# Delta net stage of a six-stage kernel: block products that read the triangle itself, one relayed inverse turned on VectorE, and the inverse's chain of steps in four parts

## The chip, the cores and the metric

One Trainium2 chip, one of its cores. The metric is the device time of the whole program in microseconds, the median of several executions.

## The reference, cut to what matters

The program is a transformer piece of six stages in a row on an activation of 2 x 512 tokens x 256 channels: a mixture of experts with zero experts, an attention, the same mixture again, a mixture of eight experts with GELU, a gated delta net, and the GELU mixture again. The change touches the delta net only. For each of its 32 value heads and each chunk of 64 tokens the reference does this:

```python
decay_mask = jnp.exp(jnp.clip(g[..., :, None] - g[..., None, :], -30.0, 30.0))
decay_mask = decay_mask * jnp.tril(jnp.ones((chunk_size, chunk_size), jnp.float32))
attn = -(jnp.einsum('bhcid,bhcjd->bhcij', k_beta, k) * decay_mask)
attn = jnp.where(upper, 0.0, attn)
...
attn, _ = jax.lax.scan(_correct_row, attn, jnp.arange(1, chunk_size))
attn = attn + jnp.eye(chunk_size, dtype=attn.dtype)
value_corrected = jnp.einsum('bhcij,bhcjd->bhcid', attn, v_beta)
...
v_prime = v_c - jnp.einsum('bhld,bhde->bhle', kcd_c, state)
inter = jnp.einsum('bhld,bhde->bhle', q_c, state) * ge_c[..., None]
out = inter + jnp.einsum('bhij,bhjd->bhid', intra, v_prime)
new_state = state * gel_c[..., None] + jnp.einsum('bhld,bhle->bhde', k_c * kd_c, v_prime)
```

The row-by-row correction with the identity added is the inverse of a unit triangular 64 x 64 matrix. It must be had for each of 8 chunks x 2 sequences x 32 value heads before the chunk's new values can be formed; the state makes the chunks of a head a chain.

## The kernel before, in words

The delta net runs over 16 key heads (a "head" below), each with 2 value heads stacked on the 128 partitions. `run` (L1311) goes through one list of named steps, and every engine executes its own part of each step in that order: `prepare_order(0)`, `front_order(0, 0)` and one `pair_order` for the first head, then a loop of seven bodies of two heads (`body_order`), then one last body. Semaphore counts tie the engines together. So the order in which an engine does things is the written order, and a wait on one step holds up all that stands behind it on that engine.

A head has four pairs of chunks, and each is one call of `pair_order(done, build, front, extra)`. The call does three things side by side. It carries the state through the two chunks of `done`: `read_state` (PE L1527, L1531; DVE makes `wv`, L1879), `new_values` (PE L1546, ACT makes `vp`), `update` (PE L1560, L1564; DVE L1891 makes the new state, L1898 the output). It builds the inverses of the two chunks of `build` in two levels: `z` is a product (PE L1504) and a mask (DVE L1871, tile `zi`), `e` two products (PE L1513, L1517), copied out by ACT. And it makes the operands of the two chunks of `front`: `turn` (PE L1466, L1468), then `unit` for both chunks (POOL L1746 adds the identity to the chunk's triangle, `bi = ge + eye`) and `lower` (PE L1489: 16 products with the identity turn `bi`, ACT copies the result to `ai`). `z` takes `ai` as its stationary operand. `lower` stands at the end of a pair, right ahead of the next pair's `read_state`.

Between these fixed steps stand the `extra` slots 0 to 6, in which `body_order` (L1188) places the preparation of the next head q: the projections `proj` 0 to 11 (PE L1431, and L1438 for 8 to 11; alternately into PSUM banks A and C), the taps of a convolution (`tap`, DVE L1801 and L1804, 4 for each of 4 groups), `silu`, norms, `coefs`, `shares` (POOL L1739), and four times `gram` (PE L1478 into bank C) with `decay` (DVE L1841 and L1844, which empty bank C and write `intra` and the triangle `ge`). The call that has `done` = (j, 0) places norms and coefficients, (j, 2) the four grams, (j, 4) the rest, (j, 6) the output of head j and early work of head j + 2.

The starting blocks of the inverse, 16 x 16 each, come by a relay through DRAM. `spread` (SP L1379, L1383) stores the diagonal blocks of `ge` in 8 DMAs, waits, and loads them as `whole_blocks`, one block to a partition. `base` (DVE L1856 to L1864) inverts all blocks at once with a chain of 1 + 2 x 14 small instructions, each waiting for the one before, and a copy that turns the result. `gather` (SP L1387 to L1398) stores both results, waits for both, and issues 16 DMAs of 16 KB, 8 into `w16` and 8 into `w16t`, the inverse and its transpose in place for the products. `z` of level 0 waits for all of them (L1497), and the load of the next weights (`load_weights`, L1348, issued at `proj` 11) stands behind them in SP's order. These weights are needed by `proj` 0, slot 0 of the pair (j, 6).

```python
        yield from pair_order((j, 4), (j, 6), (q, 0) if prep else None, [
            SL("v1"), PR(8), PR(9), ONE("base") + ONE("gather") + PR(10), PR(11), [], []])
```

## Time and profile before

| | us |
|---|---|
| median of 3 runs (lowest, highest) | 3184.04 (3183.61, 3184.51) |
| the profiled execution | 3190.36 |
| its span, first to last instruction | 3188.6 |
| delta net, main loop and ends, in that span | 907 to 2783 |

The mean granted clock of TensorE over the span is 0.869 of full speed. The profile names the engines PE (TensorE; PEld is its weight load), DVE (VectorE), ACT (ScalarE), POOL (GpSimd) and SP (SyncE, which issues the DMAs). In a timeline a row is a group of equal instructions that follow each other: its start, its length, the engine, the line, what it writes and reads, how many; in brackets the engine's idle time before it and what ended that. "issue" is idle time in which no releaser was found.

### The profile page before, as it was taken

Reading aid. Unit: us, or ns where it says so; the run is one execution under the profiler, and the core shown is the slowest. Engines: PE = TensorE matmul, PEld = TensorE weight load, DVE = VectorE, ACT = ScalarE, POOL = GpSimd, SP = SyncE. Lnnn points to the kernel's source line nnn. Section 1 sums busy time; section 2 is a strip of 40 time slices with the busy share of each in tenths; the row PEclk is TensorE's granted clock in tenths of the full one; section 3 lists DMA queues with packets and bytes.
Section 4 is the critical chain, followed back from the end, with each engine's and each line's share of the span. In section 5 each row is a group of like instructions: output and inputs, shape, how many; then the busy total and the mean of one; then the engine's idle time right before and its main releaser. Section 6 shows DMA issues by size and latency. Waiting matters only on the chain. (4 is left out here: it accounts for less than half of the span.)

```text
span 3188.6 us, 60191 instructions
## 1 busy us (share of the span) xinstructions
PE 2620.2 (82%) x23890; PEld 1999.5 (63%) x23890; DVE 1616.2 (51%) x3376; ACT 1142.0 (36%) x2442; POOL 438.4 (14%) x479
## 2 busy tenths in 40 slices
PE   7899879999656778778778778777877877789998
PEld 4433559999534556556557556556655656679997
DVE  4443456766244445445455454454454544466663
ACT  1123222332134345445444444444444444323221
POOL 0011000000011122122122222222212212100000
PEclk9889889999768789789788788788888878889999
DMA  1000112010011110110110110010011000011110
GB/s 44 25 1 1 30 41 77 27 52 26 5 34 27 27 25 15 28 28 8 28 28 8 28 28 12 24 28 16 22 30 25 11 21 12 19 66 53 44 35 13
DMA packets 172725, 85.22 MB, mean 27 GB/s; under 512 B 121664, under 2 KB 162128, under 8 KB 172496
## 3 DMA queue, kind: packets, MB, share of 16 engines
q1 hardware_dynamic: 172496, 82.02, 9.8%
q8 instruction: 162, 2.65, 0.3%
q14 instruction: 67, 0.55, 0.1%
HBM read 74.51 MB, written 7.47 MB: 26 GB/s over the span
## 5 line engine op out<-in xcount | busy, mean ns | idle before, releaser
L1431 PE MATMUL dn_ps<-xnT,dn_w 128*128 128x512 f32 x512 | 298.9, 721 | 60.1 <-DMA dn_w<-in_W_qkvz_dram 41.0
L435 ACT ACTIVATE g_h<-g_ps,g_b_now 128x512 f32<-128x512 f32 x256 | 174.9, 688 | 338.4 <-PE g_ps L459 332.5
L472 PE MATMUL g_ps<-g_w_low,g_h_high 128*128 128x256 f32 x1024 | 289.8, 283 | 0.0
L472 PE MATMUL g_ps<-g_w_high,g_h_low 128*128 128x256 f32 x1024 | 289.8, 283 | 0.0
L472 PE MATMUL g_ps<-g_w_high,g_h_high 128*128 128x256 f32 x1024 | 289.7, 283 | 0.0
L1804 DVE SCALAR_TENSOR_TENSOR dn_cv<-dn_raw,dn_cw,dn_cv 128x1024 f32<-128x1024 f32 x192 | 282.3, 1470 | 5.3
L1758 POOL TENSOR_TENSOR xn<-xn,dn_zt 128x256 f32<-128x256 f32 x128 | 99.3, 776 | 1198.5 <-DVE xn L1898 856.9
L1871 DVE TENSOR_TENSOR dn_zi<-dn_ps,dn_mz 128x128 f32<-128x128 f32 x256 | 66.5, 286 | 312.4 <-PE dn_ps L1504 308.1
L459 PE MATMUL g_ps<-g_x_high,g_w_high 128*128 128x512 f32 x512 | 201.9, 394 | 17.8 <-DVE g_w_low L516 15.6
L1489 PE MATMUL dn_ps<-ident,dn_bi 64*64 64x64 f32 x1024 | 58.0, 270 | 179.1 <-POOL dn_bi L1746 174.2
L1431 PEld LDWEIGHTS dn_ps<-xnT,dn_w 128*128 128x128 f32 x512 | 103.7, 221 | 161.6 <-issue 128.2
L459 PE MATMUL g_ps<-g_x_low,g_w_high 128*128 128x512 f32 x512 | 201.2, 393 | 0.0
L459 PE MATMUL g_ps<-g_x_high,g_w_low 128*128 128x512 f32 x512 | 200.8, 392 | 0.0
L472 PEld LDWEIGHTS g_ps<-g_w_high,g_h_high 128*128 128x128 f32 x1024 | 196.5, 192 | 0.9
L472 PEld LDWEIGHTS g_ps<-g_w_low,g_h_high 128*128 128x128 f32 x1024 | 196.5, 192 | 0.9
L472 PEld LDWEIGHTS g_ps<-g_w_high,g_h_low 128*128 128x128 f32 x1024 | 196.5, 192 | 0.0
L1891 DVE TENSOR_TENSOR dn_state<-dn_kept,dn_ps 128x512 f32<-128x512 f32 x96 | 65.5, 682 | 248.3 <-PE dn_ps L1560 248.2
L516 DVE TENSOR_TENSOR g_h_low<-g_h,g_h_high 128x512 fp32r<-128x512 f32 x256 | 177.3, 693 | 8.8
L1489 PEld LDWEIGHTS dn_ps<-ident,dn_bi 64*64 64x64 f32 x1024 | 49.1, 176 | 192.9 <-issue 154.8
L1602 ACT ACTIVATE dn_raw<-dn_ps 128x512 f32<-128x512 f32 x128 | 76.2, 595 | 205.1 <-PE dn_ps L1431 205.1
L513 DVE CAST g_h_high<-g_h 128x512 fp32r<-128x512 f32 x256 | 109.0, 426 | 78.8 <-ACT g_h L435 77.8
L565 DVE SCALAR_TENSOR_TENSOR x_res<-g_ps,g_w,x_res 128x256 f32<-128x256 f32 x128 | 61.8, 483 | 171.9 <-PE g_ps L472 171.9
(270 smaller groups left out, 5482.7 us busy)
## 6 DMA issues: line engine op xcount, KB each, us to landing
g_w<-in_fc_dram SPq DMA_DIRECT2D x32, 1024.0 KB, 6.4
dn_w<-in_W_qkvz_dram SPq DMA_DIRECT2D x16, 768.0 KB, 4.4
dn_x<-dn_cum_rows SPq DMA_DIRECT2D x32, 256.0 KB, 3.9
dn_wout<-in_W_out_dram SPq DMA_DIRECT2D x16, 256.0 KB, 2.8
f_gate<-in_gateT_dram SPq DMA_DIRECT2D x16, 128.0 KB, 2.2
f_up<-in_upT_dram SPq DMA_DIRECT2D x16, 128.0 KB, 2.3
f_down<-in_downT_dram SPq DMA_DIRECT2D x16, 128.0 KB, 2.5
dn_blocks_rows<-dn_ge SPq DMA_DIRECT2D x128, 16.0 KB, 1.7
```

What stands on the lines that cost most here:

```text
L435: nc.scalar.activation(h[:, f % 4], h_b[f % 4], ACT.Gelu, bias=b1_now[u // 2][:, f:f + 1]).then_inc(h_ready, 1)
L459: last = pe.matmul(h_b[f % 4], weights[:, k, f * P:(f + 1) * P], x[:, k, half * BANK:(half + 1) * BANK], start=(k == 0 and n == 0), stop=( ...
L472: last = pe.matmul(y_b[q % 2][:, 0:D], hidden[:, f, q * P:(q + 1) * P], weights[:, f, :], start=(f == 0 and n == 0), stop=(f == NF - 1 and ...
L513: nc.vector.tensor_copy(high, whole).then_inc(high_made, 1)
L516: return nc.vector.tensor_tensor(low, whole, high.bitcast(F32), ALU.subtract)
L1431: mm = pe.matmul(to, w[:, k, W_COL[u] * P:(W_COL[u] + 1) * P], m.xnT[:, k, b * T:(b + 1) * T], start=(k == 0), stop=(k == KD - 1))
L1489: mm = pe.matmul(block_of(bA, n, b, h), bi[n][half(h), b, :], eye_of(h), start=True, stop=True)
L1602: copy = lambda out, in_, **kw: nc.scalar.activation(out, in_, ACT.Copy, **kw)
L1758: nc.gpsimd.tensor_tensor(o[:, c], o[:, c], zt[f][:, c], ALU.mult).then_inc(s_["oz_r"], 1)
L1804: ins = nc.vector.scalar_tensor_tensor(out=cv[:, u], in0=raw[:, u % 3, :, tap:tap + T], scalar=cw[:, g, tap:tap + 1], in1=cv[:, u], op0=AL ...
L1871: nc.vector.tensor_tensor(zi[s][:], thirds(bD[s], 0), over_b(mz[l]), ALU.mult).then_inc(s_["Zi_r"], 1)
L1891: nc.vector.tensor_tensor(state[:], kept[:], added_to_state, ALU.add).then_inc(s_["S_r"], 1)
```

## The change

`lower` and the tiles `bi` and `ai` go. `unit` now adds the identity to the whole head's `ge` in one POOL instruction, after the grams are done and the blocks are stored. `z` takes `ge` itself as the stationary operand and the turned inverse as the moving one, and so computes the transpose of what it computed; the masks are the transposed ones, and in `e` the two operands change places. `base` writes its inverse into `turned` through a transposed view, so the copy at its end goes; its chain is cut in four parts (7, 8, 8 and 6 instructions) placed in slot 6 of the pair (j, 2) and slots 0, 1 and 2 of (j, 4). `gather` relays only `turned` (1 store, 8 loads) and stands in slot 2. A new step `mirror` makes `w16` from `w16t` with one DVE transpose (128 x 1024, in 32 x 32 blocks) in slot 6 of (j, 4); `e` of level 0 waits for it. In the pair (j, 2) the grams stand two and two in slots 1 and 2, `spread` in slot 2, `proj` 6 in slot 0 and `proj` 7 in slot 4. Two tiles fewer are cleared at the start.

```diff
-    yield from [("base", j), ("gather", j)]
+    yield from [("base", j, n) for n in range(4)] + [("gather", j), ("unit", j), ("mirror", j)]
 def front_order(j, c):
-    yield from [("turn", j, c), ("turn", j, c + 1), ("unit", j, c), ("unit", j, c + 1), ("lower", j, c)]
+    yield from [("turn", j, c), ("turn", j, c + 1)]
...
     yield from ahead(1, "turn")
-    yield from ahead(0, "unit")
-    yield from ahead(1, "unit")
     yield from extra[5]
-    yield from ahead(0, "lower")
     yield from extra[6]
...
         yield from pair_order((j, 2), (j, 4), (j, 6), [
-            GD(0), GD(2), SL("v0") + GD(4), GD(6) + ONE("spread"), PR(6) + PR(7), TP(3, 0, 1), TP(3, 2, 3)])
+            PR(6), GD(0) + GD(2), GD(4) + GD(6) + ONE("spread"), SL("v0"), PR(7), TP(3, 0, 1), BS(0) + TP(3, 2, 3)])
         yield from pair_order((j, 4), (j, 6), (q, 0) if prep else None, [
-            SL("v1"), PR(8), PR(9), ONE("base") + ONE("gather") + PR(10), PR(11), [], []])
+            SL("v1") + BS(1), PR(8) + BS(2), PR(9) + BS(3) + ONE("gather") + ONE("unit"), PR(10), PR(11), [], ONE("mirror")])
...
+        inverse = turned[:].rearrange("p s r -> p r s")
...
                     wait(sp, "base_r", kh + 1)
-                    for tile, scratch in ((inverse, inverse_dram), (turned, turned_dram)):
-                        sp.dma_start(scratch.rearrange("h t n r s -> (h t n) (r s)"), tile[:].rearrange("p r s -> p (r s)")).then_inc(w16_stored, 16)
-                    sp.wait_ge(w16_stored, (kh + 1) * 32)
+                    sp.dma_start(turned_dram.rearrange("h t n r s -> (h t n) (r s)"), turned[:].rearrange("p r s -> p (r s)")).then_inc(w16_stored, 16)
+                    sp.wait_ge(w16_stored, (kh + 1) * 16)
                     wait(sp, "E_r", 16 * (kh - 1))
-                    wait(sp, "z16", 4)
-                    for tile, scratch in ((w16, inverse_dram), (w16t, turned_dram)):
-                        for h in range(GRP):
-                            for t in range(QUARTERS):
-                                rows = slice(h * C + t * BASE, h * C + (t + 1) * BASE)
-                                sp.dma_start(tile[f][rows, :, t * BASE:(t + 1) * BASE],
-                                             scratch[h, t].rearrange("n r s -> r n s")).then_inc(w16_loaded, 16)
+                    wait(sp, "z16", 2)
+                    for h in range(GRP):
+                        for t in range(QUARTERS):
+                            rows = slice(h * C + t * BASE, h * C + (t + 1) * BASE)
+                            sp.dma_start(w16t[f][rows, :, t * BASE:(t + 1) * BASE],
+                                         turned_dram[h, t].rearrange("n r s -> r n s")).then_inc(w16_loaded, 16)
...
-                elif name == "lower":
...
                     if l == 0:
-                        wait(pe, "AI_r", pair_count(i, j, c) + 1)
-                        pe.wait_ge(w16_loaded, (kh + 1) * 32 * GRP * QUARTERS)
+                        wait(pe, "G_r", kh + 1)
+                        pe.wait_ge(w16_loaded, (kh + 1) * 16 * GRP * QUARTERS)
...
-                            mm = pe.matmul(block_of(bD[s], 0, b, h), ai[half(h), s, b, :], inverse_of[half(h), b, :], start=True, stop=True)
+                            mm = pe.matmul(block_of(bD[s], 0, b, h), of_chunk(ge[f], c)[half(h), b, :], turned_of[half(h), b, :],
+                                           start=True, stop=True)
...
                     wait(pe, "Zi_r", level(i, j, c, l) + 1)
+                    if l == 0:
+                        wait(pe, "mirror_r", kh + 1)
                     for b in range(B):
                         for h in range(GRP):
-                            mm = pe.matmul(block_of(bD[s], 1, b, h), turned_of[half(h), b, :], zi[s][half(h), b, :], start=True, stop=True)
+                            mm = pe.matmul(block_of(bD[s], 1, b, h), zi[s][half(h), b, :], inverse_of[half(h), b, :], start=True, stop=True)
...
-                    wait(pool, "C_e", pair_count(i, j, c) + 1)
-                    wait(pool, "D0_r", pair_count(i, j, c))
-                    nc.gpsimd.tensor_tensor(bi[s][:], of_chunk(ge[f], c), over_b(eye2), ALU.add).then_inc(s_["BI_r"], 1)
+                    wait(pool, "C_e", kh * 4 + 4)
+                    pool.wait_ge(ge_stored, (kh + 1) * 16 * GRP * QUARTERS)
+                    nc.gpsimd.tensor_tensor(ge[f][:], ge[f][:], over_head(eye2), ALU.add).then_inc(s_["G_r"], 1)
...
+                    rows = BASE - 2
+                    bounds = [rows, rows - 3, rows - 7, rows - 11, 0]
...
-                    nc.vector.tensor_copy(turned[:].rearrange("p s r -> p r s"), inverse[:]).then_inc(s_["base_r"], 1)
...
+                elif name == "mirror":
+                    dve.wait_ge(w16_loaded, (kh + 1) * 16 * GRP * QUARTERS)
+                    wait(dve, "E_r", 16 * (kh - 1))
+                    whole_head = lambda t: t[:].rearrange("p n s -> p (n s)")
+                    nc.vector.transpose(whole_head(w16[f]), whole_head(w16t[f])).then_inc(s_["mirror_r"], 1)
```

## Rows read from the trace of the kernel before

**Rows 1.** Stretches: us from:to, length, busy PE, PEld, DVE, ACT, POOL, clock, DMA, GB/s.
```profile
1009.00:2687.00 1678.00, 1311.21 (x15862) 994.06 (x15859) 832.00 (x1808) 744.83 (x1778) 376.83 (x355) 0.84 0.09 21
...
1638.10:1657.20 19.10, 7.79 (x52) 4.67 (x52) 5.89 (x13) 4.49 (x9) 4.27 (x5) 0.58 0.34 76
```

**Rows 2.** Waits of the whole run: who waited for whom, us in total, times, longest.
```profile
PE dn_ps L1489 <- POOL dn_bi L1746: 174.2, 60, 3.9
PE dn_ps L1504 <- issue: 93.2, 15, 7.2
```

**Rows 3.** Timeline of PE, pairs (j, 4) and (j, 6) of one head.
```profile
1621.65 1.06 PE L1546 MATMUL dn_ps<-dn_wv,dn_winv 64*64 64x128 f32 x8
...
1636.18 0.72 PE L1560 MATMUL dn_ps<-dn_vp,dn_kdk 64*128 64x128 f32 x8
...
1641.72 1.12 PE L1489 MATMUL dn_ps<-ident,dn_bi 64*64 64x64 f32 x16 [3.66 <-POOL dn_bi L1746]
...
1650.48 1.12 PE L1504 MATMUL dn_ps<-dn_w,dn_ai 64*64 64x64 f32 x16 [5.73 <-issue]
1653.55 3.78 PE L1431 MATMUL dn_ps<-xnT,dn_w 128*128 128x512 f32 x4 [1.95 <-DMA dn_w<-in_W_qkvz_dram]
1657.26 1.09 PE L1546 MATMUL dn_ps<-dn_wv,dn_winv 64*64 64x128 f32 x8
```

**Rows 4.** Timeline of SP's queue, the same head: the gather and the weights.
```profile
1639.50 0.43 SPq L1389 DMA_DIRECT2D dn_turned_rows<-dn_turned  x1
1641.32 3.75 SPq L1397 DMA_DIRECT2D dn_w<-dn_inverse_rows  x8
1645.12 3.88 SPq L1397 DMA_DIRECT2D dn_w16t<-dn_turned_rows  x8
1649.04 0.45 SPq L1348 DMA_DIRECT2D dn_w<-in_W_qkvz_dram  x1
```

**Rows 5.** Timeline of DVE, the same head.
```profile
1615.98 4.74 DVE L1804 SCALAR_TENSOR_TENSOR dn_cv<-dn_raw,dn_cw,dn_cv 128x1024 f32<-128x1024 f32 x3
1620.63 0.60 DVE L1879 SCALAR_TENSOR_TENSOR dn_wv<-dn_ps,dn_cf,dn_vt 128x128 f32<-128x128 f32 x2
...
1627.50 0.42 DVE L1898 TENSOR_TENSOR xn<-dn_ps,dn_qs 128x256 f32<-128x256 f32 x1
...
1631.69 0.41 DVE L1856 TENSOR_TENSOR dn_inverse<-dn_whole_blocks,dn_eye 128x256 f32<-128x256 f32 x1
...
1638.73 0.38 DVE L1864 COPY dn_turned<-dn_inverse 128x256 f32<-128x256 f32 x1
...
1668.01 3.92 DVE L1804 SCALAR_TENSOR_TENSOR dn_cv<-dn_raw,dn_cw,dn_cv 128x1024 f32<-128x1024 f32 x3
```

**Rows 6.** Timeline of PE: (j, 2) of an earlier head, then this head to (j, 4).
```profile
1142.28 0.65 PE L1546 MATMUL dn_ps<-dn_wv,dn_winv 64*64 64x128 f32 x8 [1.08 <-DVE dn_wv L1879]
...
1595.27 0.68 PE L1489 MATMUL dn_ps<-ident,dn_bi 64*64 64x64 f32 x16 [1.82 <-POOL dn_bi L1746]
...
1609.17 3.70 PE L1431 MATMUL dn_ps<-xnT,dn_w 128*128 128x512 f32 x8
...
1617.79 1.12 PE L1489 MATMUL dn_ps<-ident,dn_bi 64*64 64x64 f32 x16 [3.10 <-POOL dn_bi L1746]
```

**Rows 7.** Timeline of PE in the delta net's start: gram behind gram, first `z`.
```profile
946.48 2.08 PE L1478 MATMUL dn_ps<-dn_qkk 128*128 128x128 f32 x8 [0.92 <-DVE dn_ge L1844]
...
978.62 1.12 PE L1504 MATMUL dn_ps<-dn_w,dn_ai 64*64 64x64 f32 x16 [12.70 <-DMA dn_w16t<-dn_turned_rows]
```

**Rows 8.** Groups by line: instructions whose durations serve as prices.
```profile
L1830 DVE TENSOR_TENSOR dn_x<-dn_x,dn_coef 128x1024 f32<-128x1024 f32 x16 | 19.5, 1216 | 12.5 <-DMA dn_x<-dn_cum_rows 12.5
L513 DVE CAST g_w_high<-g_w 128x1024 fp32r<-128x1024 f32 x64 | 43.8, 685 | 0.1
L1734 POOL TENSOR_TENSOR dn_nbs<-dn_strict,dn_ex 128x1024 f32<-128x1024 f32 x16 | 37.5, 2343 | 236.2 <-ACT dn_ex L1668 236.2
```

**Rows 9.** Timeline of DVE before the delta net's loop: the slowest operation per element.
```profile
884.25 1.75 DVE L1097 RECIPROCAL dng_um<-dng_um 128x256 f32<-128x256 f32 x1
```

More of the change, by code:

```diff
@@ L1198, in body_order @@
         NM = lambda *ns: [("norms", q, n) for n in ns] if prep else []
+        BS = lambda n: [("base", q, n)] if prep else []
         ONE = lambda name: [(name, q)] if prep else []
@@ L1407, in _ @@
         def _(pe):
-            so_far = {"turn": 0, "gram": 0, "lower": 0, "proj": 0, "turn_out": 0}
+            so_far = {"turn": 0, "gram": 0, "proj": 0, "turn_out": 0}
             last_bank = [None]
@@ L1424, in step @@
                         wait(pe, "A_e", i * 16 + so_far["turn"])
-                        wait(pe, "AI_r", i * 8 + so_far["lower"])
                     else:
@@ L1463, in step @@
                     wait(pe, "ev", i * 24 + so_far["proj"])
-                    wait(pe, "AI_r", i * 8 + so_far["lower"])
                     for b in range(B):
@@ L1479, in step @@
                     mm.then_inc(s_["C_r"], 1)
-                elif name == "lower":
-                    c, = a
-                    wait(pe, "A_e", i * 16 + so_far["turn"])
-                    wait(pe, "ev", i * 24 + so_far["proj"])
-                    wait(pe, "BI_r", chunk(i, j, c) + 2)
-                    for n in range(2):
-                        for b in range(B):
-                            for h in range(GRP):
-                                mm = pe.matmul(block_of(bA, n, b, h), bi[n][half(h), b, :], eye_of(h), start=True, stop=True)
-                    mm.then_inc(s_["D0_r"], 1)
                 elif name == "z":
@@ L1668, in step @@
                     nc.scalar.activation(ex[:], x0[:], ACT.Exp).then_inc(s_["E_x"], 1)
-                elif name == "lower":
-                    c, = a
-                    wait(act, "D0_r", pair_count(i, j, c) + 1)
-                    wait(act, "Z_r", level(i, j, c, 0))
-                    copy(ai[:], bA[:, 0:2 * P].rearrange("p (s b n) -> p s b n", s=2, b=B)).then_inc(s_["AI_r"], 1)
                 elif name == "e":
@@ L1760, in _ @@
             start_counts(pool, pool_sems)
-            for tile in w16 + w16t:
+            for tile in w16t:
                 nc.gpsimd.memset(tile[:], 0.0).then_inc(s_["z16"], 1)
@@ L1851, in then @@
                         made[0] += 1
-                        wait(dve, "base_c", made[0])
-                    dve.wait_ge(blocks_loaded, (kh + 1) * 16)
-                    dve.wait_ge(w16_stored, kh * 32)
-                    then(nc.vector.tensor_tensor(inverse[:], whole_blocks[:], eye16[:], ALU.add))
-                    for t in range(BASE - 2, 0, -1):
+                    if stage == 0:
+                        dve.wait_ge(blocks_loaded, (kh + 1) * 16)
+                        dve.wait_ge(w16_stored, kh * 16)
+                        then(nc.vector.tensor_tensor(inverse, whole_blocks[:], eye16[:], ALU.add))
+                    for t in range(bounds[stage], bounds[stage + 1], -1):
                         n = BASE - 1 - t
```

50 lines of the change are left out of this document (26 added, 24 removed).

## The prediction

> **What bounds the kernel now.** I read, in order, the busy time by stretch, the waits of the whole run, and then the timelines of PE, SP, DVE and POOL through one whole head. The stretches [rows 1] say that over the loop of the delta net PE is busy 1311 of 1678 us at a mean granted clock of 0.84, while DVE is busy 832 and POOL 377: no engine is full, and PE's gaps are what can be won. One stretch of 19.1 us at the seam between the pairs (j, 4) and (j, 6) holds 7.8 us of PE work at a clock of 0.58. The waits [rows 2] name two causes: PE waits 174.2 us in 60 cases for POOL's `bi` ahead of `lower`, and 93.2 us in 15 cases, up to 7.2 each, ahead of `z`, once per head.
>
> The timelines say what that second wait is. `z` stands still for 5.73 us [rows 3] while SP works off 16 gather DMAs, 3.75 and 3.88 us of issue [rows 4]; it starts 1.5 us after the last. The weights go out behind them at 1649.04, and `proj` 0 starts at 1653.55 [rows 3, 4], 4.5 us later. So the chain of that seam is: `base` (7.4 us of DVE with its copy, up to 1639.1 [rows 5]), store, 16 loads, weights, `proj` 0, `new_values`. From the end of `turn`, 1641.72 - 3.66 = 1638.06, to `new_values` at 1657.26 it takes 19.2 us [rows 3]. The delta net takes 1876 us for 16 heads, so a head has some 117 us.
>
> **The change, part by part.** I set the old times of this head beside the new order, stretch by stretch.
>
> *Seam (j, 4) to (j, 6).* `base` runs in parts. Parts 1 and 2 (8 instructions each, about 1.95 us by the chain's pace, 7.04 us for 29 [rows 5]) fit between `new_values` at 1621.65 and the new state 5.2 us later, 0.6 ahead of the output sum at 1627.50. Part 3 (6, 1.4 us) starts after the output of the first chunk, 1627.50 + 0.34, and ends at 1629.3, or 1629.9 if POOL's `unit` beside it slows it. The store goes out at 1629.9; its first load may follow 2.2 us later, as 1641.32 followed the first store shortly ahead of 1639.50 [rows 4]; 8 loads take 3.9; the last lands 1.5 later, at 1637.5. This is before `turn` ends at 1638.06, so `z` waits no more. The weights need `proj` 11, over by 1636.25 [rows 3], and go out at 1636.3 to 1637.4, 12 us earlier than now; they land 4.5 us later, at 1640.8 to 1641.9. `read_state` and `z` take 1.7 us without `lower`, up to 1639.7. `proj` 0 follows the weights, at the fast pace 1.9 us instead of 3.78, and `new_values` comes at 1642.7 to 1643.8 instead of 1657.26: a gain of 13.5 to 14.6 us, and I take 14.0. Then 0.6 more, as `new_values` and `e` behind it run at the higher clock.
>
> *Mirror.* No row shows a DVE transpose. A one-source operation on 128 x 1024 takes 0.69 us, a two-source one 1.22 [rows 8]; the dearest row per element, a reciprocal, takes 1.75 us for 256 [rows 9], 7.0 for 1024. I take 1.2, as it is an ordinary pass over 1024 elements. `mirror` follows the state update (product at 1636.18), output and sum, from 1638.5 to 1639.7; `wv` follows at 1640.3, while `new_values` can't start before 1642.7. It is hidden with 2.4 us to spare; at 7.0 us it would cost 7.0 - 1.2 - 2.4 = 3.4 us a head.
> The Trainium skill bears on this price. "Vector Engine (DVE) Microarchitecture Reference", section 3.8, says that the 32 x 32 transpose is "Pipelined to sustain one element per cycle per lane"; at the 0.96 GHz of "VectorE: DVE Perf Modes", Specifications, that is an estimate of 1.07 us and a start-up. The latter page's table of three transpose paths has 311 ns for 128 x 128, which, if each 128 columns cost so much, would make 2.5 us, an estimate. By either the sum stays; no run here shows it yet.
>
> *`unit`.* One POOL pass over 128 x 1024 takes 2.34 us [rows 8]. It stands where POOL waits for DVE anyway, and `kept`, queued behind it, is not needed before the second state update 9 us later. I cost it at nothing; if both were doubled by DVE beside them, cover of some 2 us is left.
>
> *Seam (j, 0) to (j, 2).* PE's wait of 1.82 us and `lower` go [rows 6]. But `wv` stands on DVE behind coefficients and taps, and in an earlier head `new_values` waits 1.08 us for it there, after all the waits that go [rows 6]. I give this seam no gain. `proj` 6, put there, fills the hole.
>
> *Inside the pair (j, 2).* Now this pair holds no PE wait. It loses `proj` 6 (half of 3.70 [rows 6]: 1.85) and takes the first gram (1.1 at full pace). Bank C is single, so a gram right behind a gram waits for DVE to empty it: 0.92 us in the start, where they also stand so [rows 7]. That makes two new stalls of 1.0 each with the start of the product, and 0.4 for `wv` and 0.4 for `vp`, as `silu` with its table load now stands right ahead of `vp` on ACT. Sum: -1.85 + 1.1 + 2.0 + 0.8 = +2.1.
>
> *Seam (j, 2) to (j, 4).* PE's wait of 3.10 and `lower` [rows 6] go, but DVE has the three taps of 4.74 us and then `wv` until 1621.23, and `new_values` started at 1621.65: DVE was only 0.4 us from being the bound. Now part 0 of `base`, 1.8 us, stands ahead of the last two taps. Without `bi` beside them three taps take between 3.92 and 4.74 [rows 5]; I take 4.5. `new_values` comes 1.8 - 0.4 - 0.2 = 1.2 us later than now.
>
> *Clock.* Behind each of the waits of 3 us and more the group of 16 products takes 1.12 us, against 0.68 behind the short one [rows 3, 6], so the granted clock has fallen. PE's new hole of some 6 us ahead of `new_values` in (j, 4) and of 2.6 us in (j, 2) puts such slow stretches where PE is the bound. Bounds are 0 and 2.5 us a head; I take 1.0, as one of the two will be short.
>
> *Seam (j, 6) to the next head.* DVE's scaling of the output ends the wait behind `lower` today. No gain.
>
> Sum per head: -14.0 - 0.6 + 2.1 + 1.2 + 1.0 = -10.3 us. 14 transitions give 144.2. The last, which has no weights to load, I put at 8. The last head has two more `lower` waits, which I price like the short one, 1.82 and 0.6 of products [rows 6]: 4.8. In the start `z` waits 12.70 us for the relay [rows 7]; 8 loads, a store and the copy less give 4.6. Total 161.6. Against the profiled execution, 3190.36, that is 3029; the median of the runs lies 6.3 lower, and 3184.0 - 161.6 = 3022.4.
>
> **Rivals.** *A. More is won* (chance 0.10): the clock costs nothing, the decays hide under the products between them. Then -13.3 a head, 186 for 14, 11 for the last and 9.4 for the ends, total 206, time 2978. For it: the clock of 0.58 goes with the long stall. Against it: the wait for bank C is seen in the start.
>
> *B. DVE holds the seams* (0.13): `mirror` at 7.0 us, or taps and chain parts stretched by POOL by as much. The gain falls by 3.4 a head, 51 in all: 3073. For it: DVE was 0.4 us from the bound already. Against it: it is busy half the time.
>
> *C. The relay is no earlier* (0.05): a part of `base` is held up behind another wait so that the store leaves when it does now. Then only 8 loads, one store and the copy are saved, 4.7 us, and half a microsecond of clock, against 4.3 of costs: 14 + 9 us won in all, 3161.
>
> *D. Slower* (0.04): the chain now reads and writes the inverse with a step of 16 elements in its innermost loop. If DVE pays for that, the place is the four parts, 7.1 us a head now. At three times the duration, part 0 adds 3.6 on the seam (j, 2) to (j, 4), parts 1 and 2 add 7.9 of which 0.7 is covered, part 3 adds 2.7 partly covered: 13.4 a head in all, more than the 10.3 won, so about 15 x 3.1 - 9 = 37 us slower, 3221. It decides from a factor of 2.6, where the four parts cost what is won. Against it: the copy that wrote with this very step took 0.38 us for 256 elements, less than the dense sum's 0.41 [rows 5].
>
> *E. It doesn't do what it says* (0.02): the first level waits for something else in the same place, and the gain is eaten by the grams: 3184.
>
> **How the numbers follow.** The forecast case has 0.66: 3022, the time I predict. Its own bounds are the clock (0 to 2.5), the seam (13.5 to 14.6) and the slack for DVE, together 2985 to 3055. The range 2975 to 3085 takes in A and B and leaves out C, D and E and the tails, under 2 in 10. A measurement of this kernel can tell about 0.2%, 6 us, from no change. Faster by more: 0.66 + 0.10 + 0.13 + 0.05 less a tail of 0.01, 0.93; same 0.03; slower 0.04.
>
> **What the changed profile would show.** No `lower`, and `z` in (j, 6) within 2 us of `turn`; the last w16t load lands ahead of `turn`'s end; `proj` 0 waits 1 to 2 us for the weights and is now the seam's last wait; the distance of the same step in two heads 10 us shorter; two waits of 0.9 us of a gram for `dn_ge`; `new_values` in (j, 4) released by `wv`; `mirror` of 1.2 us; chain instructions still 0.2 us. I am wrong if a head is shorter by less than 5 us, if `mirror` or the chain costs several times as much, or if PE waits for `dn_ge` no more and a head is shorter by 13 or more.

## The result, and the profile after

| | before | after |
|---|---|---|
| median of 4 runs (lowest, highest), us | 3183.82 (3175.39, 3184.51) | 3105.55 (3099.75, 3112.18) |
| ratio, 95% interval | | 0.976 (0.973 to 0.979) |
| the profiled execution: time, span | 3190.36, 3188.6 | 3099.75, 3098.0 |
| mean granted clock of TensorE over the span | 0.869 | 0.891 |

The change wins 78 us by the medians, and 91 between the two profiled executions, the second of which is the fastest of its four. I had forecast 161.6, a time of 3022 in a range of 2975 to 3085: the direction was right, the size half of what I said, and the time lies outside the range.

The busy time by stretch, over the loop of the delta net (columns as in [rows 1], which it answers to), and under it three waits of the whole run, which answer to [rows 2]:

```profile
1009.00:2600.00 1591.00, 1247.66 (x14648) 938.02 (x14645) 878.23 (x1790) 713.24 (x1697) 307.44 (x245) 0.87 0.09 20
```

```profile
PE dn_ps L1531 <- DVE dn_wv L1869: 140.8, 67, 6.4
...
PE dn_ps L1471 <- DVE dn_ge L1822: 31.1, 33, 2.2
...
PE dn_ps L1486 <- issue: 16.0, 15, 1.7
```

The waits for `bi` are gone with `lower`, and `z`'s 93.2 us of waiting have become 16.0. But PE now waits 140.8 us for `wv` (16.5 before), up to 6.4 each, and 31.1 us for bank C ahead of a gram (4.0 before).

To find where the time went I took from PE's timeline the start of all 128 `new_values` (one per chunk; L1546 before, L1531 after) and averaged their distances over the 13 full heads of the middle. Each column is the step from one `new_values` to the next, named by the pair; "to" is a seam between two pairs.

```
us per head         (j,0)  to(j,2)  (j,2)  to(j,4)  (j,4)  to(j,6)  (j,6)  to next   head
before              15.44    9.78    8.04   13.26   10.98   24.26   12.17   21.66   115.58
after               14.55    9.18   12.32   13.39   13.04   13.34   12.64   21.82   110.27
forecast change         0       0        +3.3 (two)  +1.0   -14.0    -0.6 (two)     -10.3
measured change     -0.89   -0.60   +4.28   +0.13   +2.06  -10.92   +0.47   +0.16   -5.31
```

The 14 heads from the first on won 70.4 us where 144.2 were forecast. The ends are near the forecast in sum, by errors that cancel: the first `new_values` comes 7.6 us earlier (4.6 forecast), the last transition wins 5.7 (8), the last head 6.3 (4.8). So the miss is in the middle heads: 3.1 us too little at the big seam, 1.1 to 1.2 too much given back at each of three other places, less 1.5 won in (j, 0) and behind it, where nothing was forecast.

The seam itself, in the timeline of DVE after the change (in the head that [rows 3] show of before), with POOL and SP beside it:

```profile
1606.65 0.42 DVE L1888 TENSOR_TENSOR xn<-dn_ps,dn_qs 128x256 f32<-128x256 f32 x1
1606.98 0.21 DVE L1842 TENSOR_TENSOR dn_outer<-dn_whole_blocks,dn_turned 128x36 f32<-128x36 f32 x1
1607.23 0.72 DVE L1845 TENSOR_TENSOR dn_turned<-dn_turned,dn_outer 128x36 f32<-128x36 f32 x1
1607.98 2.27 DVE L1842 TENSOR_TENSOR dn_outer<-dn_whole_blocks,dn_turned 128x26 f32<-128x26 f32 x1
1610.29 0.97 DVE L1845 TENSOR_TENSOR dn_turned<-dn_turned,dn_outer 128x26 f32<-128x26 f32 x1
1611.30 0.18 DVE L1842 TENSOR_TENSOR dn_outer<-dn_whole_blocks,dn_turned 128x14 f32<-128x14 f32 x1
```

```profile
1607.14 0.73 POOL L1736 TENSOR_TENSOR xn<-xn,dn_zt 128x256 f32<-128x256 f32 x1 [13.72 <-DVE xn L1888]
1607.83 2.36 POOL L1724 TENSOR_TENSOR dn_ge<-dn_ge,dn_eye 128x1024 f32<-128x1024 f32 x1
1610.15 1.05 POOL L1730 TENSOR_TENSOR dn_kept<-dn_state,dn_cf 128x512 f32<-128x512 f32 x1
```

```profile
1611.73 0.32 SPq L1385 DMA_DIRECT2D dn_turned_rows<-dn_turned  x1
1614.64 3.75 SPq L1392 DMA_DIRECT2D dn_w16t<-dn_turned_rows  x8
1618.44 0.45 SPq L1345 DMA_DIRECT2D dn_w<-in_W_qkvz_dram  x1
```

Read the DVE rows against the POOL rows. Part 3 of the chain should take 1.4 us. Three of its small instructions, each of some 0.2 us with no POOL instruction beside them, take 0.72, 2.27 and 0.97, and each ends within 0.1 us of the POOL instruction beside it (start plus length: 1607.87, 1610.19 and 1611.20). It is so in all heads but the first, which has no POOL work there, and the three durations repeat to 0.01 us. The store goes out at 1611.73 and the weights at 1618.44.

The other new places, in PE's timeline of the same head:

```profile
1573.16 0.65 PE L1531 MATMUL dn_ps<-dn_wv,dn_winv 64*64 64x128 f32 x8 [2.36 <-DVE dn_wv L1869]
...
1574.23 0.64 PE L1498 MATMUL dn_ps<-dn_w,dn_zi 64*64 64x64 f32 x8
...
1575.23 2.07 PE L1471 MATMUL dn_ps<-dn_qkk 128*128 128x128 f32 x8
1578.20 1.16 PE L1471 MATMUL dn_ps<-dn_qkk 128*128 128x128 f32 x8 [0.90 <-DVE dn_ge L1822]
...
1599.44 1.12 PE L1531 MATMUL dn_ps<-dn_wv,dn_winv 64*64 64x128 f32 x8 [6.36 <-DVE dn_wv L1869]
1600.34 0.63 PE L1498 MATMUL dn_ps<-dn_w,dn_zi 64*64 64x64 f32 x8
...
1602.19 3.16 PE L1432 MATMUL dn_ps<-dn_w,xnT 128*64 128x128 f32 x32
...
1623.14 3.78 PE L1425 MATMUL dn_ps<-xnT,dn_w 128*128 128x512 f32 x4 [2.60 <-DMA dn_w<-in_W_qkvz_dram]
```

The second gram of a slot waits 0.90 for the decay ahead of it, as forecast. Behind the hole (idle time) of 6.36 us, `new_values` (0.65 at the high clock), the groups of `e` (0.40) and projection 8 (1.97) all run at the lower of the clock's two levels (mean granted clock 0.54 from 1599.44 to 1605.20, then 1.00), and all of them stand ahead of the state update in PE's order. Behind the hole of 2.36 us in (j, 2), `new_values` is still fast, but `e` and the first gram are slow (0.59 from 1573.20 to 1577.30). And `proj` 0, at 1623.14, takes the 3.78 us that it took before. Before, PE's idle time of 3.10 us at the seam to (j, 4) ended at `lower`, four groups ahead of `new_values`, and `lower` was the first to run slow [rows 6].

### The profile page after: what moved, and what is told of

Same layout as the page of the kernel before. It is cut to its first block and busy times, and to the rows that moved or that the text cites. A ratio compares the mean times of both kernels' runs of the same rounds, so it can differ in the third digit from the quotient of the medians.

```text
span 3098.0 us, 57695 instructions
## 1 busy us (share of the span) xinstructions
PE 2559.7 (83%) x22866; PEld 1945.8 (63%) x22866; DVE 1673.5 (54%) x3376; ACT 1116.6 (36%) x2378; POOL 372.0 (12%) x365
## 5 line engine op out<-in xcount | busy, mean ns | idle before, releaser
L1531 PE MATMUL dn_ps<-dn_wv,dn_winv 64*64 64x128 f32 x896 | 84.7, 315 | 140.8 <-DVE dn_wv L1869 140.8
L1531 PEld LDWEIGHTS dn_ps<-dn_wv,dn_winv 64*64 64x64 f32 x896 | 53.8, 150 | 194.4 <-DVE dn_wv L1869 164.1
L1561 PE MATMUL dn_ps<-ident,xn 128*128 128x128 f32 x256 | 61.8, 405 | 101.0 <-DVE xn L1903 100.9
L1587 ACT ACTIVATE dn_kdk<-dn_ps,dn_cf 128x128 f32<-128x128 f32 x256 | 80.1, 364 | 177.2 <-PE dn_ps L1461 175.5
```

The source lines that it names most:

```text
L1531: mm = pe.matmul(bF[half(h), part(b)], winv[c % 4][half(h), b, :], right[half(h), b, :], start=True, stop=True)
L1561: mm = pe.transpose((bB, bF)[n % 2][:, part(k)], o[:, 2 * n + k // B, k % B, :], m.ident[:])
L1587: copy = lambda out, in_, **kw: nc.scalar.activation(out, in_, ACT.Copy, **kw)
```

## The experiments

Ratios are to the kernel before on the same chip, as the chips differed by some 0.3%; the changed kernel's own is 0.976. "Per head" is the sum of the columns above.

**1. The identity later.** Change of the changed kernel:

```diff
-            SL("v1") + BS(1), PR(8) + BS(2), PR(9) + BS(3) + ONE("gather") + ONE("unit"), PR(10), PR(11), [], ONE("mirror")])
+            SL("v1") + BS(1), PR(8) + BS(2), PR(9) + BS(3) + ONE("gather"), PR(10), PR(11) + ONE("unit"), [], ONE("mirror")])
...
                     pool.wait_ge(ge_stored, (kh + 1) * 16 * GRP * QUARTERS)
+                    wait(pool, "w_r", stateful(i, j - 1, 5))
```

> The changed kernel, with the identity added later: unit stands in slot 4 of (j, 4) and waits for wv of the chunk, when DVE is idle for some 4 us. Theory: in the changed kernel the last part of the chain takes 4.7 us instead of 1.5 because DVE stands still beside the one POOL instruction of 2.36 us (the second of its products took 2.27 us instead of 0.2). Then here the chain instructions of part 3 take 0.2 each, the store leaves some 3.2 us earlier, the weights go out with the end of proj 11 (2.7 us earlier), and a head is 2.5 to 5 us shorter: 3105.5 less 35 to 75, so 3030 to 3070. Rival: the chain is held by something else there (the output sum, its own semaphores, POOL's product with z); then part 3 still takes over 4 us and the time stays within 10 us of the changed kernel's 3105.5. Second rival: part 3 is short, but the weights are held by proj 11 and nothing is won, 3095 to 3110.

Measured: 3046.87, ratio 0.958 (0.955 to 0.960); 107.15 per head, the seam to (j, 6) 10.89 instead of 13.34. The chain's instructions, in the groups by line and form (two of each form a head, one of them in part 3), first of the changed kernel, then of this one:

```profile
L1842 DVE TENSOR_TENSOR dn_outer<-dn_whole_blocks,dn_turned 128x26 f32<-128x26 f32 x32 | 37.2, 1163 | 1.1
L1845 DVE TENSOR_TENSOR dn_turned<-dn_turned,dn_outer 128x26 f32<-128x26 f32 x32 | 18.0, 563 | 1.1
```

```profile
L1843 DVE TENSOR_TENSOR dn_outer<-dn_whole_blocks,dn_turned 128x26 f32<-128x26 f32 x32 | 17.5, 548 | 1.1
L1846 DVE TENSOR_TENSOR dn_turned<-dn_turned,dn_outer 128x26 f32<-128x26 f32 x32 | 6.5, 203 | 1.1
```

The two groups fall by 31.2 us, 2.0 a head, and the seam by 2.45. The theory holds, with the time in the middle of its range, though its steps were smaller than expected: against the last state update ahead of the seam the store leaves 1.8 us earlier (3.2 expected) and the weights 1.45 (2.7). `proj` 0 then starts 1.55 us earlier, and it is also faster: from its start to `new_values` it is 2.69 us in the mean of the 13 heads, instead of 3.59, and 1.91 in six of them, as in this one:

```profile
1065.31 1.98 PE L1425 MATMUL dn_ps<-xnT,dn_w 128*128 128x512 f32 x4 [1.41 <-DMA dn_w<-in_W_qkvz_dram]
```

Part 3 is still not free of POOL: the products with `zt` and `kept` hold two of its instructions for 0.73 and 0.96 us. At this seam the change is then worth 24.26 - 10.89 = 13.4 us of the 14.0 forecast.

**2. Both inverses relayed.** The changed kernel with a dense chain, the turning copy, 2 stores and 16 loads, and no `mirror`:

```diff
-                    nc.vector.transpose(whole_head(w16[f]), whole_head(w16t[f])).then_inc(s_["mirror_r"], 1)
...
+                    for tile, scratch in ((inverse, inverse_dram), (turned, turned_dram)):
+                        sp.dma_start(scratch.rearrange("h t n r s -> (h t n) (r s)"), tile[:].rearrange("p r s -> p (r s)")).then_inc(w16_stored, 16)
...
+                            nc.vector.tensor_copy(turned[:].rearrange("p s r -> p r s"), inverse[:]).then_inc(s_["base_r"], 1)
```

> The changed kernel, but both inverses relayed as before: dense chain, a turning copy at its end, 2 stores and 16 loads, no mirror; all else as in the changed kernel. Theory: of the seam's gain the smaller part comes from the mirror: the weights go out 3.9 + 0.4 us later for 8 more loads and a store, and 0.4 for the copy, so a head is 4 to 5 us longer than with the change: 3105.5 + 56 to 75, so 3160 to 3180, about the time of before. Rival: the weights are held by the end of proj 11 rather than by the gather, or the chain with a dense innermost loop is quicker; then under 2 us a head is lost, 3105 to 3135.

Measured: 3185.57, ratio 0.999 (0.997 to 1.000), 5 us past the theory's range; the seam is 17.88 instead of 13.34, a head 5.8 longer. The single relay, with the transpose that makes it possible, is what the change lives by: without it all the rest only comes out even. `mirror` itself, in the changed kernel:

```profile
L1854 DVE STREAM_TRANSPOSE dn_w<-dn_w16t 128x1024 f32<-128x1024 f32 x16 | 19.9, 1245 | 30.1 <-DMA dn_w16t<-dn_turned_rows 30.1
```

**3. The products alone.** The kernel before without `lower`, with the whole-head `unit` behind the gather, everything else in its old place:

```diff
-            SL("v1") + BS(1), PR(8) + BS(2), PR(9) + BS(3) + ONE("gather") + ONE("unit"), PR(10), PR(11), [], ONE("mirror")])
+            SL("v1"), PR(8), PR(9), BS(0) + BS(1) + BS(2) + BS(3) + ONE("gather") + ONE("unit") + PR(10), PR(11), [], []])
```

(on experiment 2, and the slots of (j, 2) as before.)

> The kernel before with one part of the change alone: the block products read the triangle itself and lower is gone, with unit for the whole head behind the gather in slot 3; the chain stands whole in slot 3, both inverses are relayed, grams and projections stand as before. Theory: PE's 174 us of waiting for bi were mostly hidden beside other holders of the same seams (wv behind DVE's taps at (j, 2) to (j, 4), the gather at (j, 4) to (j, 6), the scaling of the output at the fourth), so only 0 to 2 us a head are won: 3150 to 3184. Rival: the waits for bi were on the path; two of four of them at 2 to 3 us and their products won make 5 us a head and more, 3110 or less, and then the rest of the change has won nothing.

Measured: 3231.46, ratio 1.014 (1.013 to 1.016): slower, which neither theory had. The waits for `bi` are gone and 64 products a head with them, and a head takes 119.4 us instead of 115.6. The loss is in (j, 2), 9.56 instead of 8.04, in (j, 4), 13.09 instead of 10.98, and 1.4 in (j, 6) and the seam behind it. PE's timeline at the seam to (j, 4):

```profile
1632.78 0.68 PE L1487 MATMUL dn_ps<-dn_w16t,dn_ge 64*64 64x64 f32 x16
1638.28 1.12 PE L1530 MATMUL dn_ps<-dn_wv,dn_winv 64*64 64x128 f32 x8 [4.83 <-DVE dn_wv L1863]
1639.19 0.64 PE L1497 MATMUL dn_ps<-dn_w,dn_zi 64*64 64x64 f32 x8
...
1641.04 3.29 PE L1433 MATMUL dn_ps<-dn_w,xnT 128*64 128x128 f32 x32
```

Here `read_state` and `z` run at once, at the high clock, and the whole idle time stands right ahead of `new_values`. Then everything behind it is slow. In the kernel before PE stood idle for 3.10 us ahead of `lower`, and `lower`, `read_state` and `z` ran slow, in time that PE would have spent waiting for `wv` anyway; projection 8 was at the high clock again, as this row of the kernel before shows:

```profile
1624.24 1.97 PE L1438 MATMUL dn_ps<-dn_w,xnT 128*64 128x128 f32 x32
```

I made a theory of it and tested it:

**4. The products with no use.** Experiment 3 with the 16 products, and POOL's two additions ahead of them, put back where `lower` stood; nothing reads the result:

```diff
+    yield from ahead(0, "twin")
+    yield from ahead(1, "twin")
     yield from extra[5]
+    yield from ahead(0, "idle")
...
+                            mm = pe.matmul(block_of(bA, n, b, h), bi[n][half(h), b, :], eye_of(h), start=True, stop=True)
```

> e4_products_only with lower's 16 products left in where they stood, and POOL's two additions ahead of them (on another tile), with no use of the result: the work of before comes back on PE and POOL, not its consequences. e4 was 1.4% slower than the kernel before, although it has 16 products fewer at each of four places. Theory: those products ended PE's hole early and took the slow stretch of the clock on themselves and on read_state and z, ahead of new_values; without them it falls on e and the projection behind new_values, on the state's path. So with idle products in their place a head falls from 119.4 back to 115.5 to 117, the ratio from 1.014 to 0.995 to 1.003. Rival: e4 is slower because of its whole-head unit beside the gather or because z stands behind other waits; then the idle products and POOL's additions come on top, and the ratio is 1.014 or more.

Measured: 3202.81, ratio 1.004 (1.003 to 1.006), just above the theory's range, and 116.6 a head, inside it. The columns say it more sharply: (j, 2) 8.05 and (j, 4) 10.96, to 0.02 us what they were before. The 1.0 us a head that remains lies in the other columns.

```profile
1626.85 1.12 PE L1485 MATMUL dn_ps<-ident,dn_bi 64*64 64x64 f32 x16 [3.10 <-POOL dn_bi L1737]
1627.90 1.12 PE L1524 MATMUL dn_ps<-dn_state,dn_qkk 128*64 128x128 f32 x8
...
1630.71 1.06 PE L1543 MATMUL dn_ps<-dn_wv,dn_winv 64*64 64x128 f32 x8
...
1633.26 1.97 PE L1436 MATMUL dn_ps<-dn_w,xnT 128*64 128x128 f32 x32
```

Useless work makes the kernel 1% faster, by ending PE's idle time before the state's path begins. This is shown: the same products and waits, no result used. The rival, that the whole-head `unit` beside the gather makes experiment 3 slow, is refuted, as `unit` still stands there. How much is won by the 16 products and how much by the early end of the hole is not told apart.

**5. Grams apart.** The changed kernel, with a projection between two grams of a slot:

```diff
-            PR(6), GD(0) + GD(2), GD(4) + GD(6) + ONE("spread"), SL("v0"), PR(7), TP(3, 0, 1), BS(0) + TP(3, 2, 3)])
+            GD(0), PR(6) + GD(2), GD(4) + PR7A + GD(6) + ONE("spread"), SL("v0"), [], TP(3, 0, 1), BS(0) + TP(3, 2, 3)])
```

> The changed kernel, with the grams of (j, 2) set apart: gram 0 in slot 0, proj 6 and gram 2 in slot 1, gram 4, proj 7 (now into bank A) and gram 6 with spread in slot 2. Theory: the pair (j, 2) is 3.6 us longer than before in the changed kernel, 1.8 of it from two waits of 0.9 us of a gram for the decay ahead of it and the rest from the lower clock behind the hole of 2.4 us ahead of new_values. Then here the waits for dn_ge are gone and a head is 1.5 to 3.5 us shorter: 3055 to 3085. Rival: what is won there is given back at the next seam, where the taps and part 0 of the chain on DVE set new_values of (j, 4), since DVE has as much to do as before: then the hole ahead of that new_values grows by what the pair loses, and the time stays within 10 us of 3105.5.

Measured: 3163.96, ratio 0.993 (0.990 to 0.996), slower than the change by 1.7%: neither theory. The waits for `dn_ge` are gone, but the column of (j, 2) is 16.00, as PE's timeline shows:

```profile
1591.55 3.10 PE L1426 MATMUL dn_ps<-xnT,dn_w 128*128 128x512 f32 x4
1595.43 1.13 PE L1472 MATMUL dn_ps<-dn_qkk 128*128 128x128 f32 x8 [0.78 <-ACT dn_raw L1588]
...
1608.80 0.72 PE L1546 MATMUL dn_ps<-dn_vp,dn_kdk 64*128 64x128 f32 x8 [2.21 <-ACT dn_vp L1588]
```

A gram also waits for ACT to copy out the projection ahead of it (0.78, twice), the projections stand on the state's path, and with none left for slot 4 PE waits 2.21 us for `vp`, which stands behind `silu` on ACT.

**6. Grams as before.** Experiment 1 with the slots of (j, 2) as before, part 0 of the chain still in slot 6:

```diff
-            PR(6), GD(0) + GD(2), GD(4) + GD(6) + ONE("spread"), SL("v0"), PR(7), TP(3, 0, 1), BS(0) + TP(3, 2, 3)])
+            GD(0), GD(2), SL("v0") + GD(4), GD(6) + ONE("spread"), PR(6) + PR(7), TP(3, 0, 1), BS(0) + TP(3, 2, 3)])
```

> e1_unit_late, with the pair (j, 2) placed as before: grams in slots 0, 1, 2 and 3, spread in slot 3, proj 6 and 7 both in slot 4; part 0 of the chain stays in slot 6. Theory: two grams in one slot make the stretch between the second and third new_values of a head 12.3 us instead of 8.0 (mean of 13 heads), and nothing comes back at the next seam, which DVE's taps set at 13.3 us with one projection as with two. In e4_products_only, with the old places and without lower, that stretch took 9.56. So here a head is 2.4 us shorter than in e1_unit_late, 107.15: 3047 - 34 = 3013, range 3000 to 3025. Rival: spread stands 4 us later, so the blocks are not there when part 0 is due, part 0 holds the taps behind it, and the seam to (j, 4) grows by as much: 3040 to 3060.

Measured: 3023.61, ratio 0.945 (0.942 to 0.949). (j, 2) is 9.13 instead of 11.94, and the seam to (j, 4) 14.74 instead of 13.39: half of the gain comes back as two projections of 1.9 us delay the state update, and the taps stand behind it. So both theory and rival hold in part. Cut at the start of the state update (PE L1560 before, L1545 in the changed kernel), that seam is, in us and in the mean of the 13 heads:

```
                      second new_values of (j,2)    state update to first
                      to state update               new_values of (j,4)
before                4.68                          8.58
products alone (3)    4.68                          8.35
changed kernel        3.33                          10.06
experiment 1          3.33                          10.06
experiment 6          4.68                          10.06
```

The second half does not move with PE's filler: it is DVE's work from the state update to `wv`, part 0 included. A second projection in slot 4 costs 1.35 us ahead of it.

**7. A new order of (j, 2).** From that reading, the next kernel is experiment 1 with projection 6 and the first gram in the idle time ahead of `new_values`, and part 0 between the last two taps:

```diff
+            PR(6) + GD(0), GD(2), SL("v0") + GD(4), GD(6) + ONE("spread"), PR(7), TP(3, 0, 1), TP(3, 2) + BS(0) + TP(3, 3)])
```

> e1_unit_late with a new order in (j, 2): proj 6 and gram 0 in slot 0, grams 2, 4 and 6 singly in slots 1, 2 and 3, spread in slot 3, proj 7 alone in slot 4, and part 0 of the chain between the last two taps. Theory: slot 0 has a hole of 3.2 us for wv in e5, and proj 6 (1.9) fits into it; so the stretch inside (j, 2) stays at 9.1 as in e5, while the state product of its second chunk comes 1.9 us earlier and the DVE work behind it (taps, part 0, wv) with it: that seam goes from 14.74 to 12.9 to 13.4. A head is 1.3 to 1.8 us shorter than in e5 (105.8), 0.9453 of before goes to 0.938 to 0.941. Rival: the blocks land only 9 us after spread, part 0 waits for them and holds tap 3 and wv; nothing is won over e5, 0.943 to 0.948.

Measured: 2987.37, ratio 0.937 (0.935 to 0.939), better than expected: (j, 2) 8.04 as in the kernel before, the seam 13.06, a head 102.67.

**8. Projections 8 to 11 a slot earlier**, the first of them into the hole of 6.4 us. Experiment 1 with

```diff
+            PR(8) + SL("v1") + BS(1), PR(9) + BS(2), PR(10) + BS(3) + ONE("gather"), PR(11), ONE("unit"), [], ONE("mirror")])
```

> e1_unit_late, with proj 8 to 11 each one slot earlier in (j, 4): proj 8 in slot 0, ahead of new_values, where PE waits 6.4 us for wv. Theory of the clock: behind that hole all of PE's work goes at the lower clock for some 6 us (new_values 1.12 instead of 0.65, the four groups of e 0.63 instead of 0.40, proj 8 2.9 to 3.2 instead of 1.97), and all of it stands on the state's path. With proj 8 in the hole the slow stretch falls earlier or does not come; the stretch from that new_values to the next goes from 12.5 us to 10.5 to 11, and the weights go out no earlier, as the gather holds them: a head is 1 to 2.5 us shorter, 3012 to 3033. Rival: the hole is still 4.4 us and the slow stretch starts at new_values as before, now on proj 9: no change, 3040 to 3052.

Measured: 3044.37, ratio 0.955 (0.950 to 0.959), not to be told from experiment 1. (j, 4) grows from 12.51 to 13.90 and the seam behind it falls from 10.89 to 9.52; their sum is the same, 23.41 and 23.42.

```profile
1568.35 1.12 PE L1531 MATMUL dn_ps<-dn_wv,dn_winv 64*64 64x128 f32 x8 [4.47 <-DVE dn_wv L1870]
...
1577.39 1.97 PE L1432 MATMUL dn_ps<-dn_w,xnT 128*64 128x128 f32 x32 [1.37 <-ACT dn_vt L1587]
```

The projection fills the front of the hole; 4.47 us remain ahead of `new_values`, and the slow stretch stays on it. And a projection now stands in bank A right behind `turn`, and waits 1.37 us for ACT. The theory of the clock was not borne out, the rival was.

**9. The weights issued by ACT**, on experiment 8, and **10. all of it**, the slots of experiment 6 added to 9. SP's own `load_weights` at `proj` 11 goes, and ACT's step of `proj` 11 has:

```diff
+                    if mth == 11 and kh + 1 < HK:
+                        act.dma_start(w[:], W_qkvz[:, (kh + 1) * NCOL:(kh + 2) * NCOL].rearrange("(k p) n -> p k n", p=P)).then_inc(w_loaded, 16)
```

> e6_proj_early, with the load of the next weights issued by ACT, at its step of proj 11, instead of by SP behind the gather. Theory: after e6 proj 11 is over some 3 us before SP is through with the 8 gather loads, so the weights go out 3 us earlier, and of proj 0's wait of 1.9 us and the z behind the gather the later one remains: 1.5 to 2.5 us a head less than e6, 21 to 35 us. Rival: z of (j, 6), which stands ahead of proj 0 and needs the last w16t load, takes over the whole wait, and under 0.7 us a head is won, within 10 us of e6.

> e5, e6 and e7 together: the identity late, grams as before, proj 8 to 11 a slot earlier, weights by ACT. If the three gains are of different stretches, they add: e5's of the pair (j, 2), e6's of (j, 4) and e7's of the seam to (j, 6); the time is e7's less 30 to 38, near 2960. Rival: the later spread delays part 0, so that (j, 4) starts later and what e5 wins is lost there: e7's time within 10 us.

Measured: 3060.55, ratio 0.958 (0.954 to 0.962), and 3018.55, ratio 0.946 (0.943 to 0.949). The first is no better than experiment 8, the second no better than 6, and the forecasts of both (21 to 35 us won; near 2960) failed, the second's rival too. The waits of the whole run for the gathered blocks, in experiment 8 and then in 9:

```profile
DVE dn_w L1855 <- DMA dn_w16t<-dn_turned_rows: 9.5, 4, 7.0
```

```profile
PE dn_ps L1484 <- issue: 21.0, 14, 2.5
...
DVE dn_w L1855 <- DMA dn_w16t<-dn_turned_rows: 34.5, 15, 7.0
```

The wait for the weights is gone from the loop (39.5 us in 15 cases, now one in the start), but with the 768 KB on their way beside them the 16 KB loads land later, 2.6 us after issue instead of 1.9 in the median, and `mirror` and `z` wait instead: the rival's picture. The seam falls by 0.5 us only, to 9.03. (j, 2) is 1.1 longer, which the edit does not touch and the runs don't explain; it scatters by 1.3 us from head to head.

**11. The banks exchanged**, on experiments 7 and 8: projections 8 and 10 in C, 9 and 11 in A.

```diff
+            PB(8, "C") + SL("v1") + BS(1), PB(9, "A") + BS(2), PB(10, "C") + BS(3) + ONE("gather"), PB(11, "A"), ONE("unit"), [], ONE("mirror")])
```

> e9 with proj 8 to 11 a slot earlier, as in e6, and the two banks exchanged (8 and 10 in C, 9 and 11 in A). In e6 the projection behind turn stood in turn's own bank and waited 1.37 us for ACT to empty it, and the stretch inside (j, 4) grew from 12.5 to 13.9 while the next seam fell from 10.9 to 9.5. Theory: with the banks exchanged this wait is gone, the stretch inside (j, 4) is 12.5 again and the seam stays at 9.5: 1.4 us a head less than e9, about 0.006 of before less. Rival: another projection now waits for its bank in turn, and it is e9's ratio within 0.003.

Measured: 2994.36, ratio 0.940 (0.936 to 0.943), the same as experiment 7's: the wait for the bank is gone and (j, 4) is 12.29, but the seam is 11.19 again. I had read experiment 8's two columns as two effects, of which I could keep one. Their sum is 23.41, 23.48, 23.42 and 23.49 in experiments 1, 7, 8 and 11. Part 3, and with it the relay and the weights, follows the first state update of (j, 4), and what is won on PE behind that update is lost again in waiting for the relay. From `new_values` to that update these four take 5.42, 5.30, 5.36 and 5.20 us.

**12. Projection 8 timed.** On experiment 11, one wait:

```diff
+                    if mth == 8 and j:
+                        wait(pe, "base_c", kh * 28 + 1)
```

> e10 with one more wait: proj 8, in slot 0 of (j, 4), waits for the first instruction of part 0 of the chain, so that PE's idle time of some 4.6 us ahead of new_values is cut in two, proj 8 in the midst. Theory: the clock falls behind a hole of 3 us and more (new_values 1.12 instead of 0.65, e 0.63 instead of 0.40, proj 3.1 instead of 1.97), so with two holes under 3 us the work behind new_values goes at the high clock, or the slow stretch falls on proj 8 itself: new_values to the next 1.5 to 2.5 us shorter, 0.006 to 0.011 of before less than e10. Rival: the clock falls with the mean of PE's work and not with one hole; then it is e10's ratio within 0.003, and the products behind new_values stay at 1.12 and 0.63.

Measured: 2965.75, ratio 0.929 (0.927 to 0.932), 0.010 less than 11; (j, 4) is 10.67 instead of 12.29, and from `new_values` to the first state update it is 3.57 instead of 5.20. A wait that delays PE's work wins 29 us:

```profile
1543.70 3.07 PE L1435 MATMUL dn_ps<-dn_w,xnT 128*64 128x128 f32 x32 [3.58 <-DVE dn_turned L1840]
1546.70 1.12 PE L1534 MATMUL dn_ps<-dn_wv,dn_winv 64*64 64x128 f32 x8
1547.61 0.49 PE L1501 MATMUL dn_ps<-dn_w,dn_zi 64*64 64x64 f32 x8
1547.93 0.40 PE L1505 MATMUL dn_ps<-dn_zi,dn_w 64*64 64x64 f32 x8
...
1548.73 1.97 PE L1435 MATMUL dn_ps<-dn_w,xnT 128*64 128x128 f32 x32
```

Behind the hole of 3.58 the clock is still low, but it is projection 8 that pays, ahead of `new_values` (1.12, still slow); most of `e` and projection 9 are fast again. That is the second of the two ways in which the theory could come true. Its premise, a hole of 3 us and more, is too narrow: in the changed kernel the first gram is slow behind the hole of 2.36 us in 8 of 13 heads. It is the fastest kernel of this study, 4.8% under the changed one, and still computes the whole of what the reference does.

## Why the prediction was wrong in its size

**The relay seam (forecast -14.0, measured -10.92): the failed step is "I cost it at nothing", of `unit`.** I had seen that it stands beside part 3 and gave it 0.6 us ("or 1629.9 if POOL's `unit` beside it slows it"), from the thought that two engines share time in proportion. The trace shows instead that a DVE instruction with both inputs in SBUF stands still for the whole rest of the POOL instruction, however small it is: 0.2 us became 2.27. Experiment 1 moves `unit` away: 2.45 us come back at the seam, 3.12 over the whole head. By the two ratios (0.976 and 0.958) that is 59 of the 83 us that the forecast missed; without this one stall the time would have been in the range, near 3049, an estimate from experiment 1's ratio.

The Trainium skill has the rule. "SBUF — State Buffer", section "Who interferes with whom", says that "A DVE instruction with two SBUF inputs contends with a GpSimd instruction that reads SBUF", that the shared ports are an exclusive lock, and, of DVE's 2-port modes, that the engine that comes second "fully blocks". The trace agrees, and shows the full block for these additions too. It agrees also in what is not held: over the whole run `zi` and `wv`, with one input from PSUM, take the same beside a POOL instruction as without one, 0.28 and 0.34 us each. It was there to be read before; with the 2.34 us of `unit` [rows 8] the sum by it would have been some 2 us a head less, an estimate.

**The same seam, second: "`proj` 0 follows the weights, at the fast pace 1.9 us instead of 3.78".** The forecast column of 10.3 us is made of 2.95 to the last state update, 5.4 from there to `proj` 0, and 1.9. Measured (means of 13 heads) are 2.95, 6.81 and 3.59. So 1.4 of the missing 3.1 us is the late start, and 1.7 is the slow clock, which did not change at all (3.62 before): PE still stands idle for 1.35 and 2.60 us right ahead of `proj` 0. Experiment 1 has 5.26, about as forecast, and 2.69. That is also why the -0.6 behind it, for `new_values` and `e` "at the higher clock", came out at +0.63.

**The pair (j, 2) and the seam to (j, 4) (forecast +3.3, measured +4.41).** The two stalls for bank C were of 0.90, about as priced. Two terms failed. The forecast's one term for the clock, 1.0, was meant for both holes together, and (j, 2) alone used about as much: behind the hole of 2.36 us the first gram took 2.07 instead of 1.16 in the head shown, and so in 8 of 13 heads. And the projection taken out of slot 4 saved 1.35 us instead of 1.85, while DVE's way from the state update to `wv` grew by 1.48 (8.58 to 10.06) instead of 1.2, so that the seam has +0.13 where these two terms make -0.65. The gram order was the costly part of the change: experiment 7 undoes it and has 8.04 again.

**The clock (forecast +1.0, measured +2.06 in (j, 4)).** I bounded it by 0 and 2.5 us a head and took the lower half, "as one of the two will be short". The short one lowered the clock too, in most heads, as above. The long one was 6.36 us in every one of the 13 heads, and the stretch from `new_values` to the state update, in which the slow work stands, grew by 1.78; the other 0.27 lies behind it, beside `unit`, and is gone in experiment 1. The step that failed is deeper: I treated `lower` as work whose removal can only win. Experiments 3 and 4 show that its removal alone costs 1.4% and that idle products give 1.0% of it back. Which products pay for the slow stretch is decided by where PE's idle time ends, and the change moved that end to right ahead of `new_values`.

**Right were:** `mirror`, 1.2 us forecast, 1245 ns measured; the same section of the Trainium skill's "Vector Engine (DVE) Microarchitecture Reference" that I named, 3.8, is borne out with its estimate of 1.07 us and a start-up, and the 2.5 us estimated from the table is not. `z` waits no more than 1.7 us (7.2 before), though I had forecast no wait. The strided chain costs little: 0.25 us an instruction of the longest form, 0.22 before. The rivals C, D and E are refuted: the relay is earlier, the strided chain is not dear, and heads are shorter. The two columns that I gave nothing won 1.5 us a head. Of that the 0.60 at the seam to (j, 2) goes with `lower`: the two kernels that have such products there show 9.78 and 9.96, all others 9.17 to 9.67. The 0.89 in (j, 0) is no finding, as that column lies between 14.27 and 15.98 in 14 kernels that do the same there.

Rival B had "taps and chain parts stretched by POOL" as its second form, at 3.4 us a head and a chance of 0.13. Its mechanism, a chain part held beside POOL, is what happened, and near its size (3.12 us a head by experiment 1). The slow clock came on top, past its 3073. So the mechanism had been seen, and was set aside because DVE "is busy half the time", which says nothing of the place where the two engines meet.

## What to carry to other kernels

A chain of tiny DVE steps with both inputs in SBUF, put beside one long POOL pass, costs the length of that pass; move the pass to where DVE is idle. Where PE must stand idle, let the idle time end ahead of the serial path, with filler or with real work that is made to wait, because the slow clock falls on what stands next behind it. And when filler is moved, cut the stretch at the point up to which PE sets it: here the moved projection won 1.35 us ahead of the state update and part 0 cost 1.48 behind it, which the sum of +0.13 hides.

## What the runs showed of the hardware

That DVE is held for the whole of a POOL instruction, not slowed in proportion, I had not expected: in part 3, 0.72, 2.27 and 0.97 us instead of 0.2 each, every one ending with the POOL instruction beside it. The one spread that I can't place is on SP: in experiment 1 the 8 gather loads took between 3.75 and 4.91 us to issue. And with a transfer of 768 KB beside them, 16 KB loads land 0.7 us later in the median (2.6 instead of 1.9).
